# Router's scores on four column groups, in a kernel of two attention and two feed-forward layers on one core

## The reference

```python
x = x + _L0_xattn_ref(ctx_1024, _layernorm(x), mask, ...)        # 8 heads of 64, q and k l2-normalised, layernorm on the result
x = x + _L0_ffn_ref(_layernorm(x), weight_q, weight_scale, bias) # tokens rounded to int8 by their own scale, an int8 matmul
x = x + _L1_xattn_ref(_layernorm(x), ctx_1024, We, W2)           # softmax over the 128 tokens, res @ W2.T
x = x + _L1_ffn_ref(_layernorm(x), Wr, br, W1, b1, W2, b2)       # 8 experts, each token goes to one
...
    logits = xf @ Wr.T + br                    # router: 8 scores for each token
    expert_idx = jnp.argmax(logits, axis=-1)
```

## Time and profile before

| | |
|---|---|
| median of 3 runs | 961.88 us (961.7 to 963.22) |
| the profiled execution | 963.69 us, its span 962.0 us |
| busy: PE, its weight loads, DVE, ACT, POOL | 95%, 83%, 78%, 72%, 48% of the span |
| mean granted TensorE clock | 0.996 of full speed |

### The profile page before, as it was taken

How to read it: one execution, slowest core, us unless ns; L and a number is a source line. 1 busy time by engine, 2 the same in 40 slices (tenths; PEclk the granted TensorE clock), 3 DMA queues, 4 the chain that set the end, 5 groups by cost and what they waited for, 6 DMA issues and landing times.

```text
span 962.0 us, 30865 instructions
## 1 busy us (share of the span) xinstructions
PE 913.5 (95%) x11222; PEld 802.9 (83%) x11222; DVE 748.6 (78%) x2524; ACT 691.3 (72%) x1655; POOL 464.9 (48%) x1093
## 2 busy tenths in 40 slices
PE   3899999999999999999999999999999999899997
PEld 2688888888888888888888888888888878899997
DVE  4666788888888888888888888888888878868553
ACT  2777778777777777777777777777778766676764
POOL 4333333454545454544454444445453544767554
PEclk9999999999999999999999999999999999999999
DMA  6742000000000000000000000000000012246310
GB/s 180 219 132 38 2 3 1 3 13 3 13 2 13 3 10 5 14 2 8 7 11 5 8 7 8 7 8 8 8 8 7 8 47 70 60 90 111 96 52 21
DMA packets 45195, 31.45 MB, mean 33 GB/s; under 512 B 11556, under 2 KB 40167, under 8 KB 45047
## 3 DMA queue, kind: packets, MB, share of 16 engines
q1 hardware_dynamic: 39446, 19.93, 8.9%
q0 software_dynamic: 4320, 8.50, 2.8%
q10 hardware_dynamic: 1280, 1.05, 0.4%
HBM read 17.75 MB, written 12.17 MB: 31 GB/s over the span
## 4 chain that ended last, share of the span: by engine, by line
PE 69%; DVE 15%; ACT 9%; issue 3%; POOL 2%; SPq 1%; DMA 0%; DVEq 0%; POOLq 0%; ACTq 0%
PE ps L1622 9%; PE ps L1579 7%; PE ps L1554 7%; PE ps L1668 7%; PE ps L1533 5%; PE ps L1541 5%; PE ps L1376 5%; PE ps L1378 5%; PE ps L1377 5%; DVE sumsq L1271 4%; PE ps L1627 3%; ACT qk_hat L595 2%; PE ps L1652 2%; ACT probs L588 2%; PE ps L1415 1%
## 5 line engine op out<-in xcount | busy, mean ns | idle before, releaser
L1579 PE MATMUL ps<-v_x,prob 128*64 128x65 f32 x2048 | 130.6, 227 | 6.3 <-ACT qq_t L646 2.8
L655 ACT ACTIVATE prob<-ps,neg_shift 128x512 f32<-128x512 f32 x128 | 88.4, 691 | 67.0 <-PE ps L1622 66.8
L1271 DVE TENSOR_REDUCE sumsq<-qk_hat 128x8 f32<-128x512 f32 x168 | 108.4, 678 | 32.9 <-ACT qk_hat L595 30.6
L1303 DVE TENSOR_TENSOR qk_hat<-ps,rstd 128x512 f32<-128x512 f32 x168 | 106.3, 684 | 33.5 <-POOL rstd L826 32.6
L819 POOL TENSOR_TENSOR rs_t<-rs_y 128x32 f32<-128x32 f32 x73 | 17.7, 242 | 226.3 <-ACT rs_y L634 226.3
L1579 PEld LDWEIGHTS ps<-v_x,prob 128*64 128x64 f32 x2048 | 104.9, 137 | 25.2 <-issue 14.1
L1579 PE MATMUL ps<-v_c,prob 128*64 128x65 f32 x2048 | 125.7, 222 | 0.0
L1376 PE MATMUL ps<-w_hi,xc_hi 128*128 128x512 f32 x272 | 119.0, 438 | 2.4 <-POOL xc_lo L793 2.4
L595 ACT ACTIVATE qk_hat<-ps 128x512 f32<-128x512 f32 x168 | 98.7, 599 | 29.9 <-PE ps L1378 22.5
L1622 PE MATMUL ps<-qT_all,kT_all 64*128 64x128 f32 x1536 | 111.6, 285 | 2.9 <-ACT w_all L604 1.2
L1378 PE MATMUL ps<-w_hi,xc_lo 128*128 128x512 f32 x272 | 107.6, 395 | 0.0
(11 more groups left out here) (237 smaller groups left out, 2260.5 us busy)
## 6 DMA issues: line engine op xcount, KB each, us to landing
x_res<-sorted_rows SPq DMA_DIRECT2D x71, 65.5 KB
w_all<-in_L_ffn_W_dram SPq DMA_DIRECT2D x16, 256.0 KB, 4.8
sorted_rows<-fill SPq DMA_DIRECT2D x8, 327.5 KB
out_dram<-prob,x_res POOLq DMA_INDIRECT x71, 2.3
sorted_rows<-stage,idx POOLq DMA_INDIRECT x64, 2.4
ctx_res<-in_ctx_dram SPq DMA_DIRECT2D x8, 115.5 KB
x_res<-in_x_dram SPq DMA_DIRECT2D x1, 768.0 KB
sorted_rows<-fill SPq DMA_DIRECT2D x1, 524.0 KB, 5.1
```

What stands on the lines that cost most here:

```text
L655: nc.scalar.activation(prob[:, n // 2, n % 2 * INNER:(n % 2 + 1) * INNER], ps_s[n], ACT.Exp, bias=(mask_now[:, par:par + 1] if n > 1 else ...
L1271: nc.vector.reduce_sum(sumsq[:, n * H:(n + 1) * H], sq[:, n * INNER:(n + 1) * INNER].rearrange("p (h d) -> p h d", d=DH), AX).then_inc(ss_ ...
L1303: nc.vector.tensor_tensor(qk_hat[:, n * INNER:(n + 1) * INNER].rearrange("p (h d) -> p h d", d=DH), ps_qk[:, n, :].rearrange("p (h d) -> p ...
L1579: last = nc.tensor.matmul(dst[half:half + DH, :], prob[:, kt, col + half:col + half + DH], v, start=kt == 0, stop=kt == 1)
```

## The change

The router's weights are widened with zeros to 32 columns and made the stationary operand; the tokens stream. Each sequence of the group writes 32 of the 128 partitions (`ps[32 * i:32 * i + 32, 3, 0:P]`). ACT copies that to lg_t, and PE transposes it back in slot_b, behind the v products. On DVE the four instructions of t_b, which stood behind the router's steps, are laid between them. Place is added before the sums of squares. The quantised tokens' transposes go from slot_c to right behind the first q and k product, and ACT's copy of them behind its first square; in the tail both stay where they were. The fences of DVE and POOL go (nine lines; one of them is shown). PE's fence stays.

```diff
@@ -137,7 +137,7 @@
-        wr_t = sb("wr_t", [P, E])
+        wr_t = sb("wr_t", [P, 32])
@@ -180,6 +180,7 @@
+        lg_t = sb("lg_t", [P, P])
@@ -466,7 +467,7 @@
-                            (wr_t[:, :], Wr.rearrange("e d -> d e")),
+                            (wr_t[:, 0:E], Wr.rearrange("e d -> d e")),
@@ -574,6 +575,10 @@
+                if rho == 0 and group(g - 2, inside):
...
+                    after(act, "lt_done", g - 2, inside)
+                    nc.scalar.activation(lg_t[:, :], ps[:, 3, 0:P], ACT.Copy).then_inc(s["lt_copied"], 1)
@@ -588,12 +593,20 @@
                     last.then_inc(s["pr_done"], 1)
+                def quantised_copied():
+                    if rho == 2 and group(g, inside):
+                        after(act, "qT_done", g, inside)
+                        nc.scalar.activation(qq_t[:, :, :], g_qt, ACT.Copy).then_inc(s["qt_copied"], 1)
...
                                              ACT.Square).then_inc(sq_done, 1 if n == 0 or fresh(pos + 1) else 2)
+                        if n == 0:
+                            quantised_copied()
                 if tail(j, inside):
@@ -636,14 +649,12 @@
+                if not has(j + 1, inside):
+                    quantised_copied()
...
-                if rho == 2 and group(g, inside):
...
-                    after(act, "qT_done", g, inside)
-                    nc.scalar.activation(qq_t[:, :, :], g_qt, ACT.Copy).then_inc(s["qt_copied"], 1)
@@ -726,6 +737,7 @@
+            nc.gpsimd.memset(wr_t[:, :], 0.0)
@@ -786,7 +796,6 @@
-                        pool.sem_inc(s["fence_p"], 1)
@@ -1020,17 +1029,34 @@
+                    bias_all = br_b[:, :].unsqueeze(1).to_broadcast([P, G, E])
+                    if group(g - 1, inside):
+                        dve.wait_ge(rs_ready, chain(j - 1, inside))
...
+                    def centred_tokens(i):
+                        if group(g - 1, inside):
+                            last = nc.vector.tensor_scalar(t_b[:, i, :], one(x_res, G * (g - 1) + i), stat_b[:, i, 0:1],
+                                                           rstd[:, last_stat, 28 + i:29 + i], ALU.subtract, ALU.mult)
+                            if i == G - 1:
+                                last.then_inc(s["tb_done"], 1)
...
+                    centred_tokens(0)
...
-                        bias_all = br_b[:, :].unsqueeze(1).to_broadcast([P, G, E])
-                        nc.vector.tensor_tensor(lg[:, :, :], g_small.rearrange("p (g e) -> p g e", e=E), bias_all,
+                        nc.vector.tensor_tensor(lg[:, :, :], ps[:, 3, P:2 * P].rearrange("p (g w) -> p g w", w=32)[:, :, 0:E], bias_all,
...
+                    centred_tokens(1)
+                    if group(g - 2, inside):
...
+                    centred_tokens(2)
+                    if group(g - 2, inside):
...
+                    centred_tokens(3)
+                    if group(g - 2, inside):
@@ -1040,13 +1066,6 @@
-                    if group(g - 1, inside):
...
-                        dve.wait_ge(rs_ready, chain(j - 1, inside))
-                        for i in range(G):
-                            last = nc.vector.tensor_scalar(t_b[:, i, :], one(x_res, G * (g - 1) + i), stat_b[:, i, 0:1],
-                                                           rstd[:, last_stat, 28 + i:29 + i], ALU.subtract, ALU.mult)
-                        last.then_inc(s["tb_done"], 1)
@@ -1106,25 +1124,27 @@
-                        dve.sem_inc(s["fence_v"], 1)
...
-                        dve.sem_inc(s["fence_v"], 1)
...
-            def later(j, par, rho, g, inside):
...
-                last_stat = 1 - par
+            def places(j, rho, g, inside):
...
+            def later(j, par, rho, g, inside):
...
+                last_stat = 1 - par
+                if rho == 0 and group(g - 2, inside):
@@ -1260,9 +1278,12 @@
+                        places(j, rho, g, inside)
...
+                if not tail(j, inside):
+                    places(j, rho, g, inside)
@@ -1403,9 +1423,9 @@
-                        last = nc.tensor.matmul(g_small[:, i * E:(i + 1) * E], tc_t[:, i, :], wr_t[:, :],
+                        last = nc.tensor.matmul(ps[32 * i:32 * i + 32, 3, 0:P], wr_t[:, :], tc_t[:, i, :],
...
-                    last.then_inc(s["lg_done"], 1)
+                    last.then_inc(s["lt_done"], 1)
@@ -1429,6 +1449,10 @@
+                if rho == 0 and group(g - 2, inside):
...
+                    after(pe, "lt_copied", g - 2, inside)
+                    nc.tensor.transpose(ps[:, 3, P:2 * P], lg_t[:, :], ident[:, :]).then_inc(s["lg_done"], 1)
@@ -1479,13 +1503,6 @@
-                if rho == 2 and group(g, inside):
...
-                    after(pe, "q2_done", g, inside)
-                    after(pe, "x3_done", g - 1, inside)
-                    for i in range(G):
-                        last = nc.tensor.transpose(g_qt[:, i, :], q_bf[:, i, :], ident_bf[:, :])
-                    last.then_inc(s["qT_done"], 1)
@@ -1495,6 +1512,15 @@
+            def quantised(j, rho, g, inside):
...
+                if rho == 2 and group(g, inside):
...
+                    after(pe, "q2_done", g, inside)
+                    after(pe, "x3_done", g - 1, inside)
+                    for i in range(G):
+                        last = nc.tensor.transpose(g_qt[:, i, :], q_bf[:, i, :], ident_bf[:, :])
+                    last.then_inc(s["qT_done"], 1)
@@ -1592,6 +1618,10 @@
                         last.then_inc(qk_done, 1 if n == 0 or fresh(pos + 1) else 2)
+                        if n == 0:
+                            quantised(j, rho, g, inside)
+                else:
+                    quantised(j, rho, g, inside)
                 slot_c(j, rho, g, inside)
...
```

More of the change, by code:

```diff
@@ L287, in whole @@
         names = ("setup_d", "setup_t", "setup_c", "routed", "b_in", "wT_done", "w_copied", "w_taken", "tot_done", "tot_copied",
-                 "a_bn", "a_mv", "fence_v", "fence_p", "fence_t", "b_bn", "b_mv", "c_bn", "c_mv",
+                 "a_bn", "a_mv", "fence_t", "lt_done", "lt_copied", "b_bn", "b_mv", "c_bn", "c_mv",
                  "ta_done", "amax_done", "step_done", "inv_done", "q1_done", "q2_done", "qT_done", "qt_copied",
```

## The result

| | before | after |
|---|---|---|
| median | 962.46 us (4 runs, 961.7 to 963.22) | 956.25 us (4 runs, 955.51 to 956.91) |
| ratio, 95% interval | | 0.9934 (0.9921 to 0.9946) |
| the profiled execution, its span | 963.69, 962.0 us | 956.35, 954.6 us |
| mean granted clock | 0.996 | 0.998 |

Faster by 6.2 us; the forecast was 7.0 (954.9 us), in its range of 951.5 to 961. The profiled execution was forecast at 956.7 us and took 956.35. The sum is right; two of its terms are not. The profiled execution of before, 963.69 us, is slower than all four timed ones, so a comparison of the two traces shows some 1.2 us more than the medians do.

A forecast was written before the change was run, and what follows sets the result against it. The prediction took PE as the bound, with 69% of the chain. Its terms, 5.2 + 2.2 - 0.7 + 0.3 = 7.0 us, took the median from 961.9 to 954.9 us; range 951.5 to 961.

The forecast's parts named there:

- Quantised tokens moved up: Phase 2, before the tail: PE's 0.42 us stall behind qq_t goes, less 0.05 charged; gain 14 x 0.37 = 5.2 us.
- That covers it by over 1 us: Phase 2: DVE writes qk_hat's first block until 559.5, PE reads it from 560.9, so the later root makes no wait.
- Phase 3 of j mod 8 = 5: At o_n: PE is 0.42 us early, DVE only 0.1; charged 0.1 us x 7 = 0.7 us lost.
- rival 1: PE's wait moves to o_n or ACT's exponentials; half of phase 2's gain returns, about 958 us; chance 0.17.
- Rival 2: No change: DVE's path takes all, o_n late in phase 3 (-5.2), one-hot later (-1.0); 961 us; chance 0.12.
- Scores on four column groups: Router's scores: 0.45 us instead of 0.79, plus a 0.11 us transpose; net gain 0.23 us where nothing waits.
- Rival 3: Slower: column groups run one after another, scores cost 1.10 us, 0.65 more than assumed; 964.7 us; chance 0.09.
- A rounds: Rounds j mod 8 = 2 (one v product, three qk products), 6 before the tail; forecast gain 0.13 + 0.23 = 0.36 us.
- The one-hot, places: Later scores delay the one-hot; earlier place removes stalls of 0.23 and 0.36 us; together a gain of 2.2 us.
- B rounds: Rounds j mod 8 = 6 (two v, two qk products), 7 before the tail; forecast -0.4 + 0.36, about 0.
- Fences: Taken out, they give DVE some 0.5 us in phases 2 and 3, where PE does not wait.
- The tail: Fences gain some 0.5 us, later scores lose 0.2: gain 0.3 us; the 1.2 GHz stretch taken as unchanged.

The follow-up runs named there:

- q_v_early: Kernel before with the quantised tokens' transposes and copy moved up, and phase 2's v_c copies ahead of DVE's wait for the root: ratio 0.9977 to before.
- v_early_t_mid: Kernel after with lg_t's transpose between the two v products and phase 2's v_c copies ahead of DVE's wait for the root: ratio 0.9869 to before.
- p_only: Kernel before with only place added ahead of the sums of squares: ratio 0.9958 to before, 4.1 us faster.
- q_only: Kernel before with only the quantised tokens' transposes and ACT's copy of them moved up: ratio 1.0035 to before, 3.4 us slower.
- f_only: Kernel before without its nine DVE and POOL fences, nothing else: ratio 0.9983 to before, 1.7 us faster.
- with_fences: Kernel after with the nine DVE and POOL fences put back: ratio 1.0003 to before.
- v_late: Kernel after with phase 2's two v_c copies moved behind o_c of the next round: ratio 0.9959 to before, 2.8 us slower than after.

## Why the prediction was right, and where it was not

- *Quantised tokens moved up: right in its rounds, and the step failed behind them.* Forecast 14 x 0.37 = 5.2 us; rounds 0 and 4 give 7 x (0.31 + 0.40) = 5.0. The step that failed is "That covers it by over 1 us": it asked only whether qk_hat comes in time, and it does. But DVE's lead over PE falls from 2.88 to 2.19 us in round 5, and the same root also starts DVE's way to o_c, which was already being waited for. Round 5 gives back 7 x 0.53 = 3.7 us; in q_v_early and v_early_t_mid taking one item of DVE's out of that stretch gave it back.
- *Phase 3 of j mod 8 = 5: the right round, the wrong place, a fifth of the size.* I charged 0.1 us x 7 = 0.7 at o_n; o_n's waits stayed (6.2 us, before 6.3), o_c's grew. This is near rival 1's reason, that DVE's path from root to root has little room, true for one of the two phase 3 rounds, with a larger loss than rival 1's 2.6. Rival 2 had all 5.2 come back at o_n: 3.7 did, elsewhere.
- *Scores on four column groups: right.* 0.46 us against 0.45, the transpose 0.11. The Trainium skill (TensorEngine Tiling (Array Packing), Key Properties) says that a change of tiling mode drains TensorE. The trace agrees in kind: the first of the scores starts 0.20 us after the last transpose where 0.11 was usual, the product behind them starts 0.20 us after the last score where it was 0.11, which is why it takes 0.43 us of the chain instead of 0.33. So the 0.23 us for the layout was near: two times 0.09. The fourfold speedup that the Trainium skill's table names for 32 columns (same page, Theoretical Speedup), by itself an estimated 0.22 us for the scores, did not come. Rival 3 is out: the eight matmuls start 0.15 us apart from first to last.
- *The wait for lt_copied: right.* 1.1 us in 6 A rounds, up to 0.2, forecast 0.1 each.
- *The one-hot, places: right.* B rounds forecast 0, measured -0.02, with a wait of 0.8 us at the ranks (0.7 forecast); A rounds forecast -0.36, measured -0.40; p_only shows the stalls' own worth. That A comes out so well is partly luck: the moved transposes alone cost A rounds 0.55 us (q_only), a term that the sum did not have, and the other parts took it away again. A rounds wait a little for the one-hot too, 0.3 us at most, which I had at nothing.
- *Fences: too small in the rounds.* The forecast gave PE nothing in the rounds; f_only shows 0.20 us off round 5, since o_c is waited for, with 0.14 back in A rounds, and with_fences shows 2 us in all in the rounds of after.
- *The tail: the term that was off the other way.* Forecast 0.3 us, measured 2.7 in the traces and some 1.5 by the medians. The stretch at a granted clock of 0.50 was named as 1.6 us that could come or go; it is in the one trace and not in the other, with PE's wait of 1.83 us ahead of it, and that the change did this is not shown.

So 5.0 + 2.5 for the parts that were costed rightly, 3.7 instead of 0.7 back in phase 3, and 2.7 instead of 0.3 in the tail: two errors of 3.0 and 2.4 us that cancel, the second of them 1.2 by the medians. (These round lengths give 3.8 of the 4.5 us of the 64 rounds; the rest lies in the first and the last rounds.) By its total the prediction was right, by its account of phase 3 and of the tail it was not, and that the total came so near is luck.

## What to carry to other kernels

Before a wait of the bounding engine is credited as gained, look for its next wait in every later round, by the same engine's list of waits: the 3.3 us for o_c stood there, and such a wait grows by what the engine comes earlier and the other later. Where a side engine works without a pause from the event that starts it to the result that is waited for, add up this way, and set it against the time at which the bounding engine comes for the result. An item is best moved out of it into idle time (v_early_t_mid); moved only behind the first result, it made the next one late (v_late). And an edit that makes a result earlier for one engine may leave it late by the order of two of its own items: lg_t's transpose behind one product more cost 4 us (7 x 0.58), more than the column groups bring in the rounds even without this (6 x 0.18 + 7 x 0.22 = 2.6).

## What the runs showed of the hardware that was not expected

A DVE instruction of 0.34 us can take more than twice as long beside POOL's. In after, DVE's xc_hat (0.34 us in before) takes 0.80, at 556.82, while POOL works on xc_hi and xc_lo:

```profile
556.33 0.40 POOL L800 CAST xc_hi<-xc_t 128x256 fp32r<-128x256 f32 x1 [0.75 <-ACT xc_t L678]
556.81 0.73 POOL L802 TENSOR_TENSOR xc_lo<-xc_t,xc_hi 128x256 fp32r<-128x256 f32 x1
```

In round 5 this costs nothing more, since in before the copies of v_c stood there and took 1.49 us instead of 1.02. In the round ahead of A it does: in q_v_early xc_hat and its second part take 0.50 and 0.90 us where both took 0.34, because DVE comes to them 0.32 us later and so beside POOL. A small delay of an engine can be enlarged in this way by what it now runs beside. That POOL is the cause was read from the traces and not tried by itself. In rounds 8 to 60 of all fourteen traces, the 691 times that xc_hat runs with POOL idle take 0.33 to 0.35 us each, and the 471 times beside a POOL instruction 0.33 to 0.90, so it does not happen beside each of POOL's instructions.

```profile
520.92 0.50 DVE L1328 TENSOR_SCALAR xc_hat<-x_res,xc_stat,rstd 128x128 f32<-128x128 f32 x1
521.35 0.90 DVE L1328 TENSOR_SCALAR xc_hat<-ctx_res,xc_stat,rstd 128x128 f32<-128x128 f32 x1
```
